# Scores and exponentials of two heads per second step in a gated cross-attention kernel

## What is computed

```python
q_hk = (hidden_q @ Wq.T).reshape(b, s, H, K)            # H = 16 heads
q_big = jnp.einsum('bshk,hkq->bshq', q_hk, w_kc_q)
q_r = jnp.einsum('bshq,hqr->bhsr', q_big, W_qr)
k_r = jnp.einsum('bld,hdr->bhlr', kv_rope, W_kr)
scores = jnp.einsum('bhsr,bhlr->bhsl', q_r, k_r)
attn = jax.nn.softmax(scores, axis=-1)
ctx_c = jnp.einsum('bhsl,bld->bhsd', attn, kv_rope)
ctx_lat = jnp.einsum('bhsd,hkd->bshk', ctx_c, w_kc_kv)
out = ctx_lat.reshape(b, s, H * K) @ Wo.T
```

## Time and profile before

| | before |
|---|---|
| median of three runs | 470.16 us (469.36 to 470.41) |
| profiled execution | 468.57 us, span 466.7 us |
| TensorE busy | 395.1 us (85%) |
| ScalarE busy | 248.2 us (53%) |
| VectorE busy | 261.4 us (56%) |
| GpSimd busy | 135.8 us (29%) |

### The profile page before, as it was taken

The page is one execution under the profiler, slowest core; times in us unless marked ns, Lnnn a source line. Parts: engine busy times, 40 slices in busy tenths (PEclk is TensorE's granted clock), DMA queues, the critical chain, the costliest instruction groups (busy, mean ns, idle before and its releaser), DMA issues. The chain is left out here.

```text
span 466.7 us, 7900 instructions
## 1 busy us (share of the span) xinstructions
PE 395.1 (85%) x2691; PEld 328.2 (70%) x2691; DVE 261.4 (56%) x732; ACT 248.2 (53%) x507; POOL 135.8 (29%) x140
## 2 busy tenths in 40 slices
PE   1669994867988998898988898778998799999996
PEld 0335682456688777897778887678997677778885
DVE  0889434437623549624649433759762456555885
ACT  1013786437289466598484897543464354444331
POOL 4815100017001047011254011335178900001630
PEclk9999996958599999999999999999999899999999
DMA  5995700381001001020010100031264422211320
GB/s 156 303 328 186 103 2 0 117 266 44 2 23 25 2 22 25 2 47 1 1 46 3 24 23 2 1 97 47 63 204 145 146 89 73 90 46 58 103 91 23
DMA packets 30744, 35.37 MB, mean 76 GB/s; under 512 B 5713, under 2 KB 25793, under 8 KB 30449
## 3 DMA queue, kind: packets, MB, share of 16 engines
q1 hardware_dynamic: 26304, 28.11, 20.0%
q0 software_dynamic: 4400, 6.75, 6.4%
HBM read 25.61 MB, written 7.60 MB: 71 GB/s over the span
## 5 line engine op out<-in xcount | busy, mean ns | idle before, releaser
L1412 PE MATMUL bank<-kv,probs 128*128 128x128 f32 x512 | 67.6, 275 | 5.3 <-ACT negmT L1005 4.9
L1412 PEld LDWEIGHTS bank<-kv,probs 128*128 128x128 f32 x512 | 62.5, 192 | 6.2 <-issue 6.2
L1032 ACT ACTIVATE probs<-bank 128x512 f32<-128x512 f32 x64 | 37.5, 592 | 17.2 <-PE bank L1392 17.2
L1864 DVE TENSOR_REDUCE negm<-bank 128x2 f32<-128x512 f32 x64 | 41.4, 688 | 5.1 <-PE bank L1371 4.8
L1391 PE MATMUL bank<-Qs,Kh 128*128 128x256 f32 x128 | 39.0, 326 | 0.0
L1371 PE MATMUL bank<-Kh,Qs 128*128 128x256 f32 x128 | 32.3, 347 | 7.6 <-ACT fold_d L1015 3.0
L1574 PEld LDWEIGHTS bank<-W,hTs 128*128 128x128 f32 x210 | 28.1, 189 | 13.4 <-DVE hTs L2018 7.8
L936 ACT ACTIVATE gu_all<-bank 128x512 bf16<-128x512 f32 x44 | 25.9, 594 | 19.6 <-PE bank L1195 19.5
L1574 PE MATMUL bank<-W,hTs 128*128 128x256 f32 (+1 forms) x210 | 32.9, 293 | 3.8 <-DVE hTs L2018 2.6
L747 POOL TENSOR_TENSOR W<-w_in,W 128x512 fp32r<-128x512 f32 x24 | 30.0, 1279 | 21.2 <-issue 21.2
L736 POOL TENSOR_SCALAR veps<-mv 128x2 f32<-128x2 f32 x12 | 2.7, 225 | 111.2 <-DVE mv L1608 111.2
(11 more groups left out here) (209 smaller groups left out, 896.4 us busy)
## 6 DMA issues: line engine op xcount, KB each, us to landing
Qm<-Qs SPq DMA_DIRECT2D x32, 128.0 KB
xs<-f3A SPq DMA_DIRECT2D x1, 2432.0 KB, 10.2
Qm<-xs SPq DMA_DIRECT2D x19, 128.0 KB, 2.0
ys<-y SPq DMA_DIRECT2D x19, 128.0 KB, 2.0
w_q<-in_wq SPq DMA_DIRECT2D x2, 1024.0 KB, 17.8
w_o<-in_woT SPq DMA_DIRECT2D x1, 2048.0 KB, 11.2
w_in<-in_L_ffn_Wg SPq DMA_DIRECT2D x8, 256.0 KB, 4.6
w_in<-in_L_ffn_Wu SPq DMA_DIRECT2D x8, 256.0 KB, 3.1
```

The costliest lines, as they stand in the source:

```text
L1032: done(act.activation(flat(pT[:, n % 3]), bank1(b, FILL_ST + h)[:], ACT.Exp), "p_ready")
L1412: ins = pe.matmul(bank_v(b, h // 2)[:, at:at + P], pT[:, n % 3, lt, t * P:(t + 1) * P], kv_all[:, frm:frm + P], start=(lt == 0), stop=(lt ...
L1864: done(dve.tensor_reduce(negm[:, :, max_at(h)], rows(bank1(b, FILL_S + h)), AX.X, ALU.max, negate=True), "m_ready")
```

## The change

The even steps of the second phase no longer issue scores, exponentials or values. Each odd step h below 16 issues the scores of heads h-1 and h on TensorE and their exponentials on ScalarE, one behind the other; each odd step from 3 to 17 then issues the values of heads h-3 and h-2. The turns (`turn_max`, `turn_ctx`), the copies and VectorE's divisions keep their steps. `run_all` and the semaphores are as they were; the counts waited for are those of each head.

```diff
                 for h in range(NH + 4):
-                    if h < NH:
-                        n = NH * b + h
+                    for i in (h - 1, h) if h % 2 and h < NH else ():
+                        n = NH * b + i
                         act.wait_ge(S_["sT_ready"], n + 1)
                         if n >= 3:
                             act.wait_ge(S_["pv_ready"], n - 2)
-                        if h == 1:
+                        if i == 1:
                             copy_max(1)
-                        done(act.activation(flat(pT[:, n % 3]), bank1(b, FILL_ST + h)[:], ACT.Exp), "p_ready")
+                        done(act.activation(flat(pT[:, n % 3]), bank1(b, FILL_ST + i)[:], ACT.Exp), "p_ready")
...
                 for h in range(NH + 4):
-                    if h < NH:
+                    if h % 2 and h < NH:
+                        scores_T(h - 1)
                         scores_T(h)
                     if h == 1:
                         turn_max(1)
-                    if 2 <= h <= NH + 1:
+                    if h % 2 and 3 <= h <= NH + 1:
+                        values(h - 3)
                         values(h - 2)
```

## The result

The changed kernel took 476.76 us (median of four, 475.65 to 483.22) against 469.76 for the kernel before on the same chip: 1.0165 times as long, 95% interval 1.0091 to 1.0239. A second set of runs gave 477.58 against 470.20, 1.0139 (1.0113 to 1.0164). It is slower by 7.0 to 7.4 us. The first profile of it fell into a disturbed execution, so the trace shown here as "after" is that of the second set (477.58 us, span 475.8; the kernel is the same).

The account below looks back on a forecast made before the run. TensorE and ScalarE nearly level up to d0; cover of TensorE's waits, not any engine's rate, is what moves. 2 x (0.83 + 0.89) + 1.70 + 0.3 = 5.4 us on 470.16 gives 475.5; range 471.6 to 478.6.

Parts of the forecast that it names:

- rival B: Granted TensorE clock also falls behind batch 2's waits, costing 1.5 us: 477.0, or 478.5 if in two batches; chance 0.18.
- TensorE's own work: nothing: All paired steps: the same matmuls run, and alternating scores and values costs nothing that pairs could give back.
- rival E: Each switch between scores and values costs 0.08 us, which pairs save at 32 steps: 472.9; chance 0.04.
- Steps 0 to 11: +0.06: Second phase up to d0 (first down matmul), batches 0 to 2: new waits replace old ones, d0 0.06 us later.
- Rival D: Faster: ScalarE has no wait left, d0 comes 0.8 us early in three batches, later losses absorbed: 467.8; chance 0.10.
- After d1: +0.83: Batches 0 and 1, second to third down group: scores 12 and values 10 leave the gap; 0.83 us lost each.
- At the turn of the next f: +0.89: Batches 0 and 1, before the next feed-forward's transposes: values 14 leave a 1.43 us gap, which stays empty; 0.89 each.
- Carried over: Query matmuls to next scores: waits there hang on copies of query results, which move along, so all loss counts.
- rival C: Waits between query matmuls and scores absorb the loss: about 470.5, up to 473 with part of it; chance 0.08.
- Batch 3: +0.3: Last batch: plan 0.3 us later; TensorE about 1.0 later behind it, inside the 1.96 wait before the tiles.
- Batch 2: +1.70: After d0: third down group 0.33 us later, and scores 12 and values 10 (1.37) still owed; 1.70 in all.
- Busy time unchanged: A sign that would show the forecast: TensorE's busy time stays the same.

Follow-up runs that it names:

- the run with work in the wait: Changed kernel with the matmuls of d1 (second down group) issued three times in batch 2, ahead of d2 (third); 474.48 us, 1.0082 against the kernel before.
- the kernel with both edits: Kernel before, with heads 10 and 11 paired in batches 0 to 2 and the transposes of the next f behind step 17; 469.87 us, 0.9959.

## Why the prediction was right, and the term that was too small

The forecast was 475.5 us with a range of 471.6 to 478.6; 476.8 and 477.6 were measured, slower as expected. The times lie nearer to the 477.0 of rival B than to the forecast: the gaps came nearly as forecast, and on top of them a fall of the clock that the sum had left out. The range held the time because it took in B. The steps, one by one:

- **TensorE's own work: nothing.** Right. In batch 1, where the clock was 1.00 before and after, the stage has the same 466 matmuls; 16 values in a row still last 1.95. Where no wait stands ahead, the scores of two heads and the values of two follow each other without a gap and take as long as before (3.61 against 3.62, above); rival E is out. The Trainium skill, page "TensorE: Matmul & The Clock Gate", section "Back-to-back issue gap", has about 81 ns for a matmul of 128 columns in a sustained stream. The trace disagrees: 16 values issued from 208.06, and the next group at 209.84, make 0.111 us for each of these f32 matmuls.
- **Steps 0 to 11: +0.06.** Right in the sum: from the turned maxima to d0 28.33 us (190.43 to 218.76), 28.26 before. The waits were smaller than in the run through the order. The profile tells 1.02, 0.31 and 0.56 as idle, but the forecast counted from the spacing of starts: the scores of head 4 start 0.91 behind the group F at 202.45, which costs 0.44, so 0.47 is lost. Counted like that they are 1.17, 0.47 and 0.72, where 1.3, 0.6 and 0.8 were given. Rival D (d0 0.8 early) didn't come.
- **After d1: +0.83.** 0.70 measured (from d0 to the transposes of f 16.99 us, 218.76 to 235.75; 16.29 before). d2 came 1.65 behind d0 (2.34 before) and not 1.74; 0.50 of that is told as idle, and by the spacing of starts, with 0.97 for d0 and d1 as in the forecast, the wait is 0.68 and not 0.74. The four ScalarE instructions ahead of the copy of d0 were as counted: from the exponentials at 217.82 to the copy at 219.73 it is 1.91, and 4 x 0.48 is 1.92.
- **At the turn of the next f: +0.89.** Exact: from the transposes of f to the query matmuls 4.26 us (235.75 to 240.01), 3.37 before. The gap is empty for 1.27.
- **Carried over.** Right. From the query matmuls of batch 1 to d0 of batch 2 it is 45.85 us after (240.01 to 285.86) and 45.79 before (235.10 to 280.89); rival C, which let the waits of this stage swallow the loss, is out.
- **Batch 3: +0.3.** 0.42 at the plan, and 0.07 more to the first tile. That the slack of 1.96 was enough is luck: TensorE comes 0.64 later to the 48 matmuls ahead of the tile (20.50 us behind the plan, 19.86 before; 1.0 was forecast), and the second fall, for which the sum had nothing, adds 1.53, together 2.17.
- **Batch 2: +1.70.** This is the term that was mis-sized: 3.87 measured. The gap is right (1.59 by the run with work in the wait). What the sum left out is rival B, to which the forecast gave 0.18: the granted clock falls to 0.50 behind the waits of 0.70 and 1.94. Its price was put at 1.5, from the 3.0 us at half rate in the earlier trace rows; here TensorE has a full queue for some 6.5 us at 1.2 GHz, and it costs 3.28. From the query matmuls on 1.08 comes back, because the fall that the kernel before has at 302 us doesn't occur (19.39 us to the turned maxima before, 18.31 after). 0.08 + 1.59 + 3.28 - 1.08 = 3.87.

"Busy time unchanged" was a wrong mark to set: TensorE's went from 395.1 to 401.3 us with the same 2691 matmuls, since a matmul at half the clock is busy for longer (L1210 in batch 2: 1.22 for 0.70). In batch 1, with the clock at 1.00 in both, it grew by 0.78. There a matmul with a wait behind it is counted to its end, as in front of the scores of head 4 (0.47 lost, 0.31 told as idle); that this makes up all of the 0.78 is not shown.

The reason given against B, that a wait of 1.80 had left the clock at 1.00, was weak: it looked at one wait, and the changed kernel has two within 4 us. What stays open is why the same pair of waits drops the clock in batch 0 and not in batch 1 of one kernel.

## What to carry to other kernels

In an order interleaved by hand, work that stands between a matmul group and the next one that needs its copied result is cover: before it is moved, look at what is left in each gap, and count what an empty gap costs. Where TensorE has a full queue behind such a gap, add what a fall of its clock would cost: here 3.28 us, twice the 1.59 of the gap itself. Where it has slack behind the gap, the fall can cost nothing, as it did ahead of the first tile. Work that nobody needs, put into waits that can't be shortened, was worth more here (5.7 us) than every reordering tried.

## What the hardware did that was not expected

- The clock falls after waits in which TensorE was still busy around half the time (2.06 of 4.0 us here, 1.81 of 3.0 with steps 12 and 13 paired), but not each time: 1.66 of 3.0 left it at 1.00, and so did 3.24 of 6.0 in the kernel with both edits:

```profile
298.00:304.00 6.00, 3.24 (x26) 2.60 (x25) 3.61 (x8) 2.67 (x6) 2.85 (x4) 1.00 0.00 0
```

- The same work can go either way. The turns and transposes at the end of batch 2 keep TensorE busy 1.74 of 4.0 us in both kernels; before, the clock is at 0.50 behind them, and in the changed kernel it stays:

```profile
307.84:311.84 4.00, 1.74 (x14) 1.30 (x13) 1.61 (x4) 1.58 (x3) 1.39 (x2) 1.00 0.00 0
311.84:314.84 3.00, 2.50 (x22) 2.30 (x20) 1.29 (x3) 1.17 (x2) 3.00 (x5) 1.00 0.00 0
```

Ahead of the first tile it is the other way round: 1.85 of 4.0 us busy in both, and the clock falls in the changed kernel alone.

- How long it stays low differs between executions of the same work. In batch 0 the kernel before and the one with steps 0 to 11 paired run alike up to 116 us. By stretch, the clock of the kernel before (profiled run 468.57 us) is back only at 127:

```profile
116.00:118.00 2.00, 1.64 (x8) 1.25 (x7) 1.29 (x2) 0.60 (x1) 1.15 (x1) 0.50 0.00 0
118.00:128.00 10.00, 9.27 (x38) 7.23 (x38) 6.66 (x11) 2.58 (x5) 0.00 (x0) 0.52 0.01 2
```

and that of the kernel with steps 0 to 11 paired (profiled run 465.0 us) by 118:

```profile
116.00:118.00 2.00, 1.57 (x8) 1.07 (x7) 1.41 (x3) 0.60 (x1) 1.12 (x1) 0.65 0.00 0
118.00:128.00 10.00, 7.93 (x52) 5.96 (x53) 7.24 (x13) 5.26 (x11) 0.00 (x0) 1.00 0.01 2
```

Of the 3.5 us between the spans of these two profiles (466.7 and 463.2), 2.81 stand at d0 of batch 0 (149.99 and 147.18). Both kernels have single runs of 464.7 to 465.2 us beside the many near 470, so one profile by itself says little about a change of a few us.
